# Far tiles through per-head states, one table for levels 1 to 8, a plain logit product, a ring of seven score tiles

## The reference

```
q, k, v = n Wq, n Wk, n Wv            per head, width 128
g   = -softplus(n Wg + bg);  G = cumsum(g) over tokens
lam = softplus(n Wdl + Lparam)        12 levels for each token and head
level(t,s) = 0 if t == s, else floor(log2(t-s)) + 1
A[t,s] = q_t.k_s / sqrt(128) * exp(G_t - G_s) * lam[t, level(t,s)]    for s <= t
x = x + layernorm(sum over heads of (A v) Wo + n) * ln_g + ln_b
x = x + top-2-of-8 expert mixture of layernorm(x)
```

## Time and profile before

| | |
|---|---|
| median of three runs | 1446.13 us |
| the profiled execution | 1447.56 us, span 1445.8 us |
| PE busy | 1367.9 us, 95% |
| PEld | 1156.4 us, 80% |
| ACT | 1191.5 us, 82% |
| DVE | 1046.4 us, 72% |
| POOL | 926.0 us, 64% |
| mean granted TensorE clock | 0.986 |

### The profile page before, as it was taken

How to read it: one execution, slowest core, us unless ns; L and a number is a source line. 1 busy time by engine, 2 the same in 40 slices (tenths; PEclk the granted TensorE clock), 3 DMA queues, 4 the chain that set the end, 5 groups by cost and what they waited for, 6 DMA issues and landing times.

```text
span 1445.8 us, 30362 instructions
## 1 busy us (share of the span) xinstructions
PE 1367.9 (95%) x10214; PEld 1156.4 (80%) x10214; DVE 1046.4 (72%) x2445; ACT 1191.5 (82%) x3428; POOL 926.0 (64%) x1018
## 2 busy tenths in 40 slices
PE   5799999999999999999999999999999999999997
PEld 5588888878878788788888788887887878878874
DVE  5656766687766977678766887668776697667777
ACT  3699989898889888898798988989888988888742
POOL 2255568755696567955589455875569656696573
PEclk9899999999999999999999999999999999999998
DMA  5421222213221133111321122211322112222100
GB/s 184 105 63 32 56 58 62 44 31 82 50 55 32 40 70 69 47 40 35 74 66 33 46 48 54 69 43 32 81 51 55 32 40 60 65 46 47 39 8 15
DMA packets 275062, 78.02 MB, mean 54 GB/s; under 512 B 200105, under 2 KB 264859, under 8 KB 274779
## 3 DMA queue, kind: packets, MB, share of 16 engines
q1 hardware_dynamic: 272664, 75.61, 23.2%
q10 hardware_dynamic: 2242, 0.46, 0.2%
HBM read 65.80 MB, written 9.67 MB: 52 GB/s over the span
## 4 chain that ended last, share of the span: by engine, by line
PE 53%; POOL 20%; ACT 12%; DVE 10%; issue 3%; SPq 1%; DMA 0%; ACTq 0%; POOLq 0%; DVEq 0%
PE o_ps L1467 15%; POOL a_lo L639 10%; PE s_ps L1388 6%; PE l_ps L1409 5%; PE s_ps L1390 5%; PE s_ps L1389 5%; PE aux L1388 5%; PE aux L1390 4%; PE aux L1389 4%; ACT w_all L790 3%; DVE a_all L1033 2%; ACT a_hi L824 2%; POOL e_rs L645 2%; POOL late L664 2%; ACT w_all L804 1%
## 5 line engine op out<-in xcount | busy, mean ns | idle before, releaser
L639 POOL TENSOR_TENSOR a_lo<-a_all,a_hi 128x512 fp32r<-128x512 f32 (+2 forms) x640 | 712.2, 1133 | 463.1 <-ACT a_hi L824 461.6
L1033 DVE TENSOR_TENSOR a_all<-s_ps,w_all 128x512 f32<-128x512 f32 (+3 forms) x768 | 418.8, 552 | 210.8 <-PE s_ps L1390 166.0
L790 ACT ACTIVATE w_all<-l_ps,bias 128x128 f32<-128x128 f32 x1589 | 438.3, 382 | 52.4 <-PE l_ps L1409 51.2
L1467 PE MATMUL o_ps<-a_hi,v_all 128*128 128x512 f32 (+2 forms) x1280 | 469.6, 372 | 6.5 <-POOL a_lo L639 5.9
L824 ACT ACTIVATE a_hi<-a_all 128x512 fp32r<-128x512 f32 (+2 forms) x640 | 355.1, 580 | 102.4 <-DVE a_all L1033 99.9
L1467 PEld LDWEIGHTS o_ps<-a_hi,v_all 128*128 128x128 f32 x1280 | 242.0, 189 | 44.0 <-POOL a_lo L639 16.0
L1388 PE MATMUL s_ps<-q_hi,xt_hi 128*128 128x512 f32 (+2 forms) x640 | 259.8, 406 | 5.5 <-DVE a_all L1033 5.4
L1390 PE MATMUL s_ps<-q_hi,xt_lo 128*128 128x512 f32 (+2 forms) x640 | 231.4, 362 | 0.0
L1467 PE MATMUL o_ps<-a_lo,v_all 128*128 128x512 f32 (+2 forms) x640 | 230.9, 361 | 0.0
L1389 PE MATMUL s_ps<-q_lo,xt_hi 128*128 128x512 f32 (+2 forms) x640 | 230.7, 360 | 0.0
L1388 PEld LDWEIGHTS s_ps<-q_hi,xt_hi 128*128 128x128 f32 x640 | 121.8, 190 | 17.4 <-DVE a_all L1033 8.9
(11 more groups left out here) (237 smaller groups left out, 2289.9 us busy)
## 6 DMA issues: line engine op xcount, KB each, us to landing
far<-ef_scratch SPq DMA_DIRECT2D x64, 320.0 KB, 3.2
rb<-eb_scratch SPq DMA_DIRECT2D x1016, 0.8 KB
farther<-ef_scratch SPq DMA_DIRECT2D x64, 192.0 KB, 3.8
ra<-ea_scratch SPq DMA_DIRECT2D x508, 4.0 KB, 2.0
mt<-m_scratch SPq DMA_DIRECT2D x62, 128.0 KB, 2.1
nt<-n_scratch SPq DMA_DIRECT2D x62, 128.0 KB, 3.4
tx<-in_L_attn_x SPq DMA_DIRECT2D x9, 512.0 KB, 5.8
out<-late SPq DMA_DIRECT2D x15, 256.0 KB, 3.6
```

Source lines behind the costliest of these rows:

```text
L639: pool.tensor_tensor(a_lo[r][:, 0:t1 - t0], a[r][:, 0:t1 - t0], a_hi[r][:, 0:t1 - t0].bitcast(F32), ALU.subtract).then_inc(a_lo_done, 1)
L790: last = act.activation(w[k][:, W_AT[j] + d, :].rearrange("p (f c) -> p f c", f=2), l_tiles[:, :, :, i - i0], ACT.Exp, bias=bias[b % 2][:, ...
L1033: dve.tensor_tensor(a[(n * NG + g) % NA][:, 0:t1 - t0], s_ps[:, g % 2, 0:t1 - t0], w[n % 2][:, at:at + (t1 - t0) // P, :].rearrange("p i n ...
L1467: last = pe.matmul(o, lhs[:, vr, j, :], rhs[r][:, 0:t1 - t0], start=fresh, stop=True, skip_group_check=True)
```

## The change

1. `ND = 5`: a key tile serves queries of five tiles only. Groups of the second half shrink: key 0 from 512 columns to 128 (now in `FULL`), key 1 to 256, key 2 to 384; there are three groups of each width, still 12.
2. Tiles 5 to 7 of queries get the rest through states. Values of keys 0 to 2 are kept scaled by a decay of their key (`e_key`, `high_v`); PE multiplies each key tile by them (`key_states`, place 32), DVE adds the three up one after the other into `state` (`states`, place 33), and PE multiplies by queries that DVE has scaled by the exponential of the farther row (`take_q`), at place 43, into o_ps (`state_values`). The six exponentials of farther become one of 384 columns on ACT (`farther_exps`, place 15). The row's sum is made once a batch in `run_far`.
3. A table `rc` with levels 1 to 8 serves distance 1, so that `rb` is no longer used there: 8 matmuls fewer, 8 loads more a head. SP's loads of the next head now stand behind the load of farther, which waits for `state_values` (`load_next_farther`).
4. Logits are one plain product of unsplit tokens and weights, from a copy that ACT makes (`xt_all`).
5. `LAG = 6`, a ring of seven. The tables of places are other ones.

```
-FAR = ((3, 9), (5, 10))
+ND = 5
+FAR = ((3, 9), (ND, 10))
+NS = NC - ND
+NQ = NS * P
...
+        _b = min(_lo + T // 2, (_j + ND) * P)
+        if _a < _b:
+            GROUPS.append((_j, _a, _b))
...
-LAG = 5
+LAG = 6
...
-FAR_AT = {7: 1, 10: 0}
+FAR_AT = {10: 0}
+B_AT = {15: 0}
+S_AT = {32: 0}
+C_OUT = {33: 0}
+X_AT = {43: 0}
...
-POOL_MORE = {9: [('t_dev', 0)], 29: [('xb', 0)], 41: [('dev1', 0)], 45: [('apply1', 1)], 49: [('apply1', 0)],
-             52: [('apply1', 2)], 61: [('apply1', 3)], 65: [('scale', 0), ('scale', 1)], 72: [('xb', 1)],
-             77: [('add', 0)], 80: [('add', 1)], 97: [('dev2', 0)], 109: [('apply2', 1)], 113: [('apply2', 2)],
+POOL_MORE = {5: [('t_dev', 0)], 44: [('xb', 0)], 52: [('dev1', 0), ('apply1', 1)], 57: [('apply1', 0)],
+             60: [('apply1', 2), ('apply1', 3)], 62: [('scale', 0)], 66: [('scale', 1)], 68: [('xb', 1), ('add', 0)],
+             73: [('add', 1)], 89: [('dev2', 0), ('apply2', 1)], 115: [('apply2', 2)], 274: [('total', 0)],
...
                     load_ra(sp, n, range(TA))
+                    load_rc(sp, n, range(TA))
                     load_rb(sp, n, range(TB))
...
+                def load_next_farther(n):
+                    sp.wait_ge(cq_done, n - 1)
+                    sp.wait_ge(t["stored"], EL * (n // H + 1))
+                    load_farther(sp, n)
...
+                def farther_exps(n):
+                    act.wait_ge(farther_in[n % 2], 16 * (n // 2 + 1))
+                    act.activation(farther[n % 2][:, :], farther[n % 2][:, :], ACT.Exp).then_inc(w_far_done, 1)
...
+                    if u and n >= 2:
+                        dve.wait_ge(w_far_done, n + 1)
+                        dve.tensor_tensor(farther[n % 2][:, :], bank(piece)[:, HALF - NQ:], farther[n % 2][:, :],
+                                          ALU.mult).then_inc(qw_done, 1)
...
+                    dve.tensor_copy(state[:, 0, :], at[0]).then_inc(c_done, 1)
+                    dve.wait_ge(c_done, 2 * n + 1)
+                    dve.tensor_tensor(state[:, 1, :], at[1], state[:, 0, :], ALU.add).then_inc(c_done, 1)
+                    dve.wait_ge(c_done, 2 * n + 2)
+                    dve.tensor_tensor(state[:, 2, :], at[2], state[:, 1, :], ALU.add).then_inc(freed(piece), 1)
...
-                        if d in (1, 2, 4):
+                                          (ra, rc)[d][k][:, tb, :, i0:i0 + cnt])
+                        if d in (2, 4):
...
+                    for j in range(NS):
+                        last = pe.matmul(o[:, j * P:(j + 1) * P], x_key[n // H % 2][:, j, :], v_full[:, n % 3, V_SLOT[j], :],
+                                         start=True, stop=True)
...
+                    for j in range(NS):
+                        last = pe.matmul(o_ps[:, (ND + j) * P:(ND + j + 1) * P], state[:, j, :],
+                                         farther[n % 2][:, j * P:(j + 1) * P], start=False, stop=True, skip_group_check=True)
...
-                        last = three(o[:, i * NLOG:(i + 1) * NLOG], xt_hi[b % 2][:, tok], xt_lo[b % 2][:, tok],
-                                     wcat_hi[:, :], wcat_lo[:, :])
+                        last = pe.matmul(o[:, i * NLOG:(i + 1) * NLOG], xt_all[:, tok], wcat[:, :], start=True, stop=True)
```

More of the change, by code:

```diff
@@ L52 @@
 AX = mybir.AxisListType.X
-W_AT = [sum(NC - k for k in range(j)) for j in range(NC)]
-NT = sum(NC - j for j in range(NC))
+W_AT = [sum(min(ND, NC - k) for k in range(j)) for j in range(NC)]
+NT = sum(min(ND, NC - j) for j in range(NC))
 BIAS_AT = [sum(NC - k for k in range(d)) for d in range(NC)]
@@ L162 @@
 SPLIT = [g for g in range(NG) if g not in FULL]
-FULL_KEYS = [GROUPS[g][0] for g in FULL]
+X_SLOT = sorted(GROUPS[g][0] for g in FULL)
+V_KEYS = [GROUPS[g][0] for g in FULL if GROUPS[g][0] >= NS]
+V_SLOT = {j: s for s, j in enumerate(list(range(NS)) + V_KEYS)}
+V_FULL_INC = [sum(2 if j < NS else 1 for j in (2 * u, 2 * u + 1) if j in V_SLOT) for u in range(NC // 2)]
+BIAS_STEPS = ND + 1
+BIAS_STEPS_FAR = NS + 1
 SLOTS = H * NG
@@ L224, in slot_pieces @@
         out.append((("v", (n + 1) // 2, V_AT[place]), base + [k for k in V_LOW if V_LOW[k] == V_AT[place]][0]))
+    if place in S_AT:
+        out.append((("S", n, 0), base + list(C_OUT)[0]))
     for kind, i in PE_MORE.get(4 * NG * h + place, ()):
@@ L273, in main_stage @@
         ra = [sb(f"ra{k}", [P, NTA, TA, NC], F16) for k in range(2)]
+        rc = [sb(f"rc{k}", [P, NTA, TA, NC], F16) for k in range(2)]
         rb = [sb(f"rb{k}", [KB, NTB, TB, NC], F16) for k in range(2)]
@@ L365, in main_stage @@
         aux_full, aux_free = sem("aux_full"), [sem(f"aux_free{k}") for k in range(2)]
-        t = {k: sem(f"t_{k}") for k in ("x_in st mv ve rs sh xn0 xn1 hi abs exp ln lam g lamc sums run bias lnl ell el_far el_hi "
+        t = {k: sem(f"t_{k}") for k in ("x_in st mv ve rs sh xn0 xn1 xt hi abs exp ln lam g lamc sums run run_far bias ek lnl ell el_far el_hi "
                                         "el_lo stored").split()}
@@ L958, in _ @@
                     exps(0, u)
-                for part in range(len(FAR)):
-                    far_exps(0, part)
+                farther_exps(0)
+                far_exps(0)
                 act.wait_ge(s_rows, 1)
@@ L1358, in _ @@
                             take_q(n + 1, Q_OUT[place])
+                        if n == 0 and Q_OUT.get(place) == 1:
+                            for k in range(2):
+                                dve.wait_ge(m_in[k], 16)
+                            dve.wait_ge(s_mst, 16)
+                            first_query(1, late[:, 1, 0:NQ])
+                        if place in C_OUT:
+                            states(n)
                         if n % 2 and place in V_LOW and n + 1 < NH:
```

332 lines of the change are left out of this document (216 added, 116 removed), and 14 rows, old and new, of tables (DVE_MORE, PE_MORE).

## The result

The changed kernel takes 1450.15 us (median of 20 runs, 1445.80 to 1455.01); the kernel before, beside it, 1446.12 (20 runs, 1444.31 to 1447.42). The ratio is 1.0024, 95% interval 1.0016 to 1.0032: slower by 0.24%. The forecast was 1385, the range 1328 to 1436. The profiled execution has a span of 1448.2 us at a mean granted clock of 0.970 (0.986 before).

A forecast was written before the change was run, and what follows sets the result against it. Each engine bounds its own stretch, PE heads 5 to 7. PE work -1.21 us a head; batch 151.7 + 12.5 waits = 164.2, 7.5 less; six batches at -7.5, two at -8: -61, so 1385 us, range 1328 to 1436.

The forecast's parts named there:

- the 1.32 a head: PE's added state work: three products of keys by values and three of state by query, 6 x 0.22 us.
- POOL's bunch: Head 1: moved mean, power and applies give POOL about 27 us while PE needs 19.3.
- Sum of waits 12.5, batch 151.7 + 12.5 = 164.2: PE's waits per batch (4.5 heads 0 to 2, 3 head 3, 5 head 4) plus its own work: 7.5 us less.
- waits 3, as before: Head 3: ACT falls from 23.04 to about 22 us, PE is 20.4; PE waits 3, before 3.5.
- Beside the batches: First head's time and tail: both 0, with ends -3 and +5 us for the start, -2 and +2 for the tail.
- So nobody waits: SP's queue: level tables behind the far load are needed over 20 us later, so the new waits cost nothing.
- B: Rival: saving swallowed in heads 1 to 4; waits 18, batch 169.7, 1431 us; chance 0.13.
- C: Rival: DVE holds the two score banks and stops PE 1.7 us a head; 32 slower, 1479 us; chance 0.07.
- D: Rival: nothing moves, PE waits for tables at SP's pace, 20 to 21 us a head; 1440 to 1450; chance 0.04.
- A: Rival: waits shrink too, 5 of the 10.3 us go; batch 156.7, 1328 us; chance 0.13.
- O: Theory of the follow-up runs, not the prediction: the pieces stand in a wrong order for the new work.
- Q: Theory of the follow-up runs, not the prediction: SP's list is the cause of the missing saving.

The follow-up runs named there:

- three more places: POOL's second-norm pieces, third expert piece and its sum later, on the changed kernel with ACT, POOL and gate-step places already moved (1437.0): 1422.91 us, ratio 0.9831 to the kernel before.
- the filled stalls: Zero-weight PE products in stalls of heads 1 and 3, on the changed kernel with ACT, POOL and gate-step places moved (1437.0): 1437.11 us, ratio 0.9929 to the kernel before.

## Why the prediction was wrong

Lengths in us, means of the six middle batches, from starts of the first score product on DVE; the forecast is own work plus waits of the text:

| stretch | before | own work, forecast | forecast | after | three more places |
|---|---|---|---|---|---|
| heads 0 to 2 | 62.4 | 52.7 | 57.2 | 60.8 | 59.5 |
| head 3 | 25.0 | 20.4 | 23.4 | 25.8 | 24.7 |
| head 4 | 21.7 | 17.7 | 22.7 | 23.4 | 22.0 |
| heads 5 to 7 | 62.6 | 60.9 | 60.9 | 61.5 | 61.4 |
| batch | 171.7 | 151.7 | 164.2 | 171.5 | 167.6 |

The 60.9 is what the other stretches leave of the text's 151.7.

*PE's work, right in its prices.* The state path taken out gave the 1.32 a head back in heads 5 to 7. That these came within 0.6 of the forecast is in part luck: the text's waits before (5.7, 3.5 and 2.2) add up to 11.4, over its own 10.3, which makes its work for heads 5 to 7 some 1 us too high. From the 62.6 before, three times 1.21 less one expert piece (0.70) that moved in gives 59.7; the run shows 61.5. Head 6, put at about 18, has 20.9: the windows are cut on DVE's products, and head 6's holds 32 products of the `ra` table where heads 5 and 7 have none, so only the sum of the three compares. In the changed kernel six key products and the six state products span 0.59 and 0.67:

```profile
810.05 0.83 PE L1619 MATMUL aux<-v_full,x_key 128*128 128x128 f32 x6
810.64 0.36 PE L1606 MATMUL o_ps<-a_hi,v_all 128*128 128x256 f32 x1
...
813.82 0.83 PE L1628 MATMUL o_ps<-farther,state 128*128 128x128 f32 x6
814.49 0.39 PE L1580 MATMUL s_ps<-q_full,x_full 128*128 128x128 f32 x2
```

*The other engines' sums, right within some 5%.* POOL's 51.2 for heads 0 to 2 is 52.1, ACT's 22 for head 3 is 22.4, DVE's 22.6 for head 4 is 21.4. POOL's bunch was put wrong: of the 52.1, 20.9 lie in head 1, where the text had 27.

*The step that failed is "Sum of waits 12.5, batch 151.7 + 12.5 = 164.2".* By the text's own prices for the work it is 19.8. I went through the stretches by each engine's busy sum in a head and took the wait from how far one stands above PE's work. That gave head 4 nearly right (5 became 5.7, with DVE at 95%). In heads 0 to 3 the sums came as forecast and the waits did not: they came from where inside a head the work stands. In head 1 ACT's exponentials stood behind shifts that the tables had moved there (4.5 became 8.1 for heads 0 to 2); in head 3 a bank waited for a low part behind softplus, guard and gates, some of it stretched beside POOL ("waits 3, as before" became 5.4). Heads 5 to 7, put at none, have 0.6. My text listed these moves for POOL and the expert sums only, and never asked what stands ahead of the two things that PE needs back at once, `l_ps` and a spare bank.

*Beside the batches.* The start came 1.8 later, inside the text's ends of -3 and +5. The first batch was to lose 8 and is 1.6 longer; from the start of the last batch to the end was to lose 8 and loses 0.2.

*"So nobody waits" on SP's queue failed* in a smaller way: the level tables were in time, but store and residual, queued behind them, were late by some 4 us for ACT and POOL (14.9 against 10.5 into the batch, from the issue at 741.28 before), and the far tile has little slack.

*The clock was not in the sum.* Same head, same instructions, two batches of the changed kernel:

```profile
236.30:259.00 22.70, 20.23 (x172) 17.87 (x171) 15.28 (x37) 20.29 (x63) 20.36 (x30) 1.00 0.30 58
...
406.30:431.80 25.50, 21.67 (x172) 19.37 (x171) 15.23 (x37) 20.57 (x63) 20.89 (x30) 0.93 0.34 76
```

PE's busy time differs by 1.4; the stall ahead of the second level unit differs by as much (2.30 in the first, 3.76 in the second). Runs of the changed kernel spread over 9 us where those before spread over 3, and the clock goes with it: of the 20, the seven with a mean granted clock of 0.973 or 0.974 average 1448.0 us, the eight with 0.970 or less 1452.3. Which of the two, stall or clock, leads is not shown: that the stalls set the half clock off is read from their order in the trace, and the filled stalls, which were of 2.0 us at most, show only that there the clock gave nothing back.

*The rivals.* B (saving swallowed in heads 1 to 4, waits of 18) had the place and nearly the size; its 0.13 was too little, and I let it end at 1431 where two more microseconds of waits make a loss. C's sign came, its mechanism didn't: the chains of heads 5 and 6 name DVE (expert sums, L1382, 5.1% and 8.8%), but PE's waits at the score banks for DVE's product are 9.3 us in the run, against 6.6; after, then before (total, times, longest):

```profile
PE s_ps L1526 <- DVE a_all L1152: 5.7, 9, 1.1
PE s_ps L1580 <- DVE a_all L1152: 3.6, 1, 3.6
```

```profile
PE s_ps L1388 <- DVE a_all L1033: 5.4, 6, 0.9
PE s_ps L1441 <- DVE a_all L1033: 1.2, 7, 0.2
```

D's sign, level products waiting for loads in mid-run, did not come (3.8 us, once, in the first head). Two sums of the text are off without moving the forecast: A's 156.7 is 157.0 (5 of 10.3 leave 5.3), and 1.1 in seven batches is 7.7, not 7 at most.

*What stays open.* O holds for 27 us: places alone took the changed kernel from 1450 to 1423, 1.7% under the kernel before. That is 3.9 of the 7.3 us a batch between forecast and result. Whether the rest to 164 a batch is to be had by a better order, or is held by one `l_ps` region and two spare banks, no run settles: a second region and a ring of eight tiles were not tried. Q is open as well: the one other order of SP's list lost by the far tile, before it could show what the late store and residual cost. Nor did a run move the places of the kernel before, so how much of the 1.7% is owed to the new work and how much to the places is not known; the table `rc` and the plain logits were not taken out by themselves.

## What to carry to other kernels

A saving on the leading engine is worth its size only in stretches where that engine is the bound; elsewhere price, from the program order of each queue, what stands ahead of the one thing that the leader needs back next. After a change of work the places of all small pieces are part of the change: here they were worth from +92 to -27 us, more than the 77 at which the whole saving on PE was priced. Moving a piece to remove a wait mostly moves the wait; look first at what the same releaser holds up next.

## What the runs showed of the hardware

The decay column copy, for which the text weighed 0.2 against 1.3, took 167 to 174 ns in all eight batches; no POOL instruction ran beside it. Another small SBUF-to-SBUF step on DVE did meet POOL: 182 to 189 ns in four of eight batches, 735 to 745 in four. Timeline of DVE, then of POOL, in one of the latter:

```profile
484.12 0.74 DVE L1209 TENSOR_SCALAR run<-sums 128x64 f32<-128x64 f32 x1
```

```profile
483.09 1.71 POOL L694 TENSOR_TENSOR a_lo_all<-a_all,a_hi 128x384 fp32r<-128x384 f32 x2 [2.62 <-ACT a_hi L894]
```

DVE's step ends at 484.85, just after POOL's second subtraction (484.80); in all four batches it ends 0.05 us after one. The guard step (L1196) does so in six batches, and the gate step (L1355) ends 0.08 us after one in seven. So its price is not a fixed 1.1 but the rest of the POOL instruction that it meets. The Trainium skill (Advanced Engine Details and Errata, Mode Summary) has GpSimd and two-port VectorE instructions block each other on the shared port; the trace agrees, with the wait bounded by one POOL instruction here. The text weighed this cost for the copy, which never paid it, and not for the guard step, where it stood ahead of PE's longest wait in head 3.
